# A two-layer program on one core: routing one attention body nearer, one activation table, pads on two queues, expert weights scaled on ScalarE

## What is computed

```python
h = layernorm(x) * (1 + ca) + sa
q = softplus(h @ Wq.T + bq); k = softplus(h @ Wk.T + bk); v = h @ Wv.T + bv      # 16 heads of 8
kv = cumsum(k[..., :, None] * v[..., None, :]); k1 = cumsum(k)
x = x + ga * ((q . kv) / (q . k1)) @ Wo.T + ...
h = layernorm(x) * (1 + cb) + sb
t = h * rsqrt(mean(h * h) + 1e-5) * norm_scale
top_v, top_i = top_k(t @ gate_w + gate_b, 2); probs = softmax(top_v)
for each expert e:  acc += w[:, e] * (swiglu(t @ w1[e] + b1[e]) @ w2[e] + b2[e])
x = x + gb * (h + acc)
```

## Time and profile before

| | us |
|---|---|
| median of 3 runs | 1131.31 (1131.22 to 1132.76) |
| profiled execution, first to last instruction | 1130.5 |
| layer 0 | 0 to 404 |
| attention and routing, bodies overlapping | 404 to 753 |
| run-out: routing of the last bodies | 753 to 797 |
| pads, plan, last scatters | 797 to 818 |
| expert stage | 818 to 1091 |
| sum and store | 1091 to 1131 |

### The profile page before, as it was taken

The page is one execution under the profiler, slowest core; times in us unless marked ns, Lnnn a source line. Parts: engine busy times, 40 slices in busy tenths (PEclk is TensorE's granted clock), DMA queues, the critical chain, the costliest instruction groups (busy, mean ns, idle before and its releaser), DMA issues.

```text
span 1130.5 us, 21078 instructions
## 1 busy us (share of the span) xinstructions
PE 904.8 (80%) x6543; PEld 700.5 (62%) x6543; DVE 863.6 (76%) x2224; ACT 682.1 (60%) x1756; POOL 563.3 (50%) x567
## 2 busy tenths in 40 slices
PE   4997799279999949999999999942088888888820
PEld 4994377134445438888888888831077777777710
DVE  2776788789998866788999999955467777676748
ACT  1357510689996376688988987755055555555510
POOL 1121000656885224433888888856635655555530
PEclk9999899579999969999999999975589999999975
DMA  7000233123333132000101111111242222222148
GB/s 191 14 1 5 75 112 112 52 85 132 123 118 113 75 102 51 2 8 9 42 32 39 38 37 40 35 37 45 82 131 72 82 71 77 79 68 77 45 165 307
DMA packets 72002, 84.37 MB, mean 75 GB/s; under 512 B 18182, under 2 KB 59841, under 8 KB 69716
## 3 DMA queue, kind: packets, MB, share of 16 engines
q1 hardware_dynamic: 52564, 60.60, 17.1%
q0 software_dynamic: 8704, 18.11, 4.8%
q10 hardware_dynamic: 10624, 4.33, 1.4%
HBM read 59.33 MB, written 23.67 MB: 73 GB/s over the span
## 4 chain that ended last, share of the span: by engine, by line
PE 39%; DVE 9%; issue 5%; ACT 4%; another core or an unknown queue 3%; DMA 1%; SPq 1%; POOL 0%; DVEq 0%; ACTq 0%; POOLq 0%
PE ps L2086 9%; PE ps L2304 9%; PE ps L2102 3%; PE ps L2323 3%; DVE qk L2003 2%; PE ps L2077 1%; PE ps L2064 1%; PE ps L2051 1%; PE ps L2097 1%; PE ps L2191 1%; PE ps L2156 1%; PE ps L2145 1%; PE ps L2209 1%; DVE qk L2008 1%
## 5 line engine op out<-in xcount | busy, mean ns | idle before, releaser
L1399 POOL DMA_INDIRECT rows_of<-payb,posu x128 | 143.2, 1119 | 53.3 <-issue 28.7
L1390 POOL TENSOR_TENSOR kvb<-qk,v 128x1024 f32<-128x1024 f32 x64 | 126.4, 1980 | 86.4 <-DVE qk L1756 53.0
L1032 PE MATMUL ps<-masked,ew 128*128 128x512 f32 x256 | 129.6, 621 | 4.2 <-DVE masked L960 3.5
L2086 PE MATMUL ps<-con,kvb 128*128 128x128 f32 x1024 | 126.9, 278 | 0.0
L2086 PEld LDWEIGHTS ps<-con,kvb 128*128 128x128 f32 x1024 | 120.4, 193 | 0.7 <-issue 0.7
L1424 POOL DMA_INDIRECT parts<-h,dest x72 | 74.0, 1028 | 72.3 <-ACT h L1658 47.2
L1649 ACT ACTIVATE nrm<-qk 128x512 f32<-128x512 f32 x72 | 45.4, 630 | 101.3 <-DVE qk L2003 87.8
L1424 POOL DMA_INDIRECT parts<-gx,dest x72 | 73.6, 1022 | 55.0 <-ACT gx L1658 33.9
L960 DVE TENSOR_TENSOR masked<-f_t,wide 128x512 f32<-128x512 f32 x128 | 88.9, 712 | 9.2 <-PE ps L1032 8.9
L1732 DVE TENSOR_TENSOR qc<-ps,qk 128x1024 f32<-128x1024 f32 x64 | 77.9, 1217 | 18.1 <-PE ps L2086 17.7
L2304 PE MATMUL ps<-qd,ex 128*128 128x256 f32 x288 | 74.4, 405 | 18.0 <-ACT ex L1634 15.8
(11 more groups left out here) (355 smaller groups left out, 2444.1 us busy)
## 6 DMA issues: line engine op xcount, KB each, us to landing
wide<-hot_dram SPq DMA_DIRECT2D x16, 1024.0 KB, 4.6
kvb<-rows_of SPq DMA_DIRECT2D x72, 132.0 KB
toep<-taps_dram SPq DMA_DIRECT2D x16, 512.0 KB, 3.8
out_dram<-x_tok ACTq DMA_DIRECT2D x16, 256.0 KB, 5.6
rows<-rows_dram SPq DMA_DIRECT2D x16, 192.0 KB, 3.1
kvb<-parts SPq DMA_DIRECT2D x6, 512.0 KB, 7.2
rows<-rows_dram SPq DMA_DIRECT2D x16, 128.0 KB, 4.4
xg<-in_w_dram SPq DMA_DIRECT2D x1, 2048.0 KB, 9.7
```

What stands on the lines that cost most here:

```text
L1032: nc.tensor.matmul(ps[:, w % 2, :], ew0[:, e, :], masked[e % 4][:, :], start=False, stop=(e == E - 1)).then_inc(s["product"], 1)
L1390: nc.gpsimd.tensor_tensor(kv[g % KB][:, :, :].rearrange("p e (h d) -> p e h d", h=H), k_in, v_in, ALU.mult).then_inc(s["kv"], 1)
L1399: nc.gpsimd.indirect_dma_start(rows_of, bass.IndirectOffsetOnAxis(ap=posu[w % 2][:, slot, t:t + 1], axis=0), pay[w % PB][:, t, :], None).t ...
L2086: last = nc.tensor.matmul(cum(g)[:, e, :], kv[g % KB][:, e, :], k("upto"), start=True, stop=True)
```

## The change

1. **Order of the loops.** The calls from `payload` on (payload, turned payload, logits, choice, ranks, places, sends) get an offset smaller by one: ACT `payload(n - 7)`, `logits_kept(n - 8)`, `weigh(n - 8)`; DVE `logits(n - 5)` to `placed(n - 5)`; PE `turn_pay(n - 5)`, `logits(n - 5)`, `ranks(n - 6)`, `logits_back(n - 6)`; POOL `send(n - 5, ...)`. Each loop has one pass less. PE's waits on shared PSUM banks are counted as they are issued, instead of by formulas with `upto_b`, and name two more semaphores; two of ACT's waits name the readers of `qk` one by one.
2. **One table.** ACT preloads the set `natural_log_exp_and_others` at the block's start; `variance_root` and `square_root` move up behind their logarithms.
3. **Pads.** SP writes 4 of the 8, ACT the other 4, each behind `place` = 1.
4. **Weights and tables.** ACT scales two experts' first weights in each of four passes (n = 7 to 10); the bias and `beside` are made by DVE in its pass n = 4 (`numbers`). The plan loses these, and one of its links: `cnt` is now computed straight from PSUM beside `base`.

```diff
@@ block.sync
-                    for e in range(E):
+                    for e in range(E // 2):
@@ block.gpsimd
-                    for n in range(B + 7):
-                        send(n - 7, 6)
+                    for n in range(B + 6):
+                        send(n - 6, 6)
                         products(n, 0)
-                        send(n - 7, 7)
-                        send(n - 6, 0)
+                        send(n - 6, 7)
+                        send(n - 5, 0)
...
@@ block.scalar
+                    def scaled_weights(q):
+                        need(act, "experts", (2 + NF) * 16)
+                        act.wait_ge(s["weights"], 3 * 16)
+                        by_e = w1b1.rearrange("p (e i) -> p e i", i=WB)[:, 2 * q:2 * q + 2, 0:I2]
+                        nc.scalar.activation(by_e, by_e, ACT.Copy, scale=ns[:, :]).then_inc(s["scaled"], 1)
...
-                    for n in range(B + 9):
+                    nc.scalar.preload_act_table_set("natural_log_exp_and_others")
+                    for n in range(B + 8):
                         abs_keys(n - 3)
...
                         variance_log(n - 6)
-                        logits_kept(n - 9)
+                        variance_root(n - 6)
+                        logits_kept(n - 8)
                         squares(n - 7)
                         logarithm(n - 3)
                         square_log(n - 7)
+                        square_root(n - 7)
                         projected(n - 5)
                         feat(n - 2)
-                        variance_root(n - 6)
-                        weigh(n - 9)
+                        weigh(n - 8)
                         spread(n - 4)
-                        payload(n - 8)
-                        square_root(n - 7)
-                        turned_pay(n - 8)
+                        payload(n - 7)
+                        turned_pay(n - 7)
...
+                        if 5 <= n - 2 <= 8:
+                            scaled_weights(n - 2 - 5)
+
+                    act.wait_ge(s["place"], 1)
+                    act.wait_ge(s["padrow"], 2)
+                    for e in range(E // 2, E):
+                        row = act.value_load(counts[0:1, e:e + 1], min_val=e * CAP, max_val=(e + 1) * CAP - SP)
+                        act.dma_start(rows_of[bass.ds(row, SP), :].rearrange("(p c) d -> p c d", c=S), far[:, :, :]).then_inc(s["pads"], 16)
                     act.wait_ge(s["place"], 2)
+                    need(act, "scaled", E // 2)
@@ block.vector
-                    for n in range(B + 6):
+                    for n in range(B + 5):
...
-                        logits(n - 6)
-                        largest(n - 6)
-                        chosen(n - 6)
+                        logits(n - 5)
+                        largest(n - 5)
+                        chosen(n - 5)
...
+                        if n == 4:
+                            numbers()
...
+                    nc.vector.tensor_scalar(cnt[:, :], ps[:, RANK, 0:E], float(SP - 1), None, ALU.add)
...
-                    link(nc.vector.scalar_tensor_tensor(cnt[:, :], k("iota"), float(-CAP), base[:, :], ALU.mult, ALU.add))
-                    link(nc.vector.tensor_scalar(cnt[:, :], cnt[:, :], float(SP - 1), None, ALU.add))
...
-                    first_weights = w1b1.rearrange("p (e i) -> p e i", i=WB)[:, :, 0:I2]
-                    nc.vector.tensor_scalar(first_weights, first_weights, ns[:, :], None, ALU.mult)
@@ block.tensor
-                    for n in range(B + 7):
-                        logits_back(n - 7)
+                    for n in range(B + 6):
+                        logits_back(n - 6)
...
-                        ranks(n - 7)
+                        ranks(n - 6)
                         sums(n - 2, 3)
-                        turn_pay(n - 6)
+                        turn_pay(n - 5)
```

More of the change, by code:

```diff
@@ L1173, in build @@
                      "pay", "pay_ps", "pay_t", "gx", "x4", "lg_ps", "lg_t", "lg_back", "lg", "max", "idx", "idf", "hot", "ed", "ee", "e1", "p1", "taken", "counted", "carried",
-                     "rank_ps", "rank", "sel", "pos", "posu", "extra", "labels", "totals", "base", "place", "pads", "experts", "plan", "padrow")
+                     "rank_ps", "rank", "sel", "pos", "posu", "extra", "labels", "totals", "base", "place", "pads", "experts", "plan", "padrow", "beside", "scaled")
             s = {nm: sem(f"p3_{nm}") for nm in names}
@@ L1934, in _ @@
                     link(nc.vector.tensor_tensor(first[:, :], upto[:, :], ntile[:, :], ALU.subtract))
-                    dve.wait_ge(s["experts"], (2 + NF) * 16)
-                    lin_bias = w1b1.rearrange("p (e i) -> p e i", i=WB)[:, :, I2 + NF // 2:WB]
-                    nc.vector.tensor_scalar(lin_bias, lin_bias, 1.0, None, ALU.add)
-                    first_weights = w1b1.rearrange("p (e i) -> p e i", i=WB)[:, :, 0:I2]
-                    nc.vector.tensor_scalar(first_weights, first_weights, ns[:, :], None, ALU.mult)
+                    need(dve, "beside", 3)
                     nc.vector.tensor_scalar(surplus[:, :], number[:, :], last_tile[:, :], NOWHERE, ALU.is_gt, ALU.mult)
-                    for half in range(S):
-                        last = nc.vector.tensor_scalar(beside[:, :, half], number[:, :], float(SP), k("token")[:, half:half + 1], ALU.mult, ALU.add)
-                    link(last)
-                    link(nc.vector.tensor_scalar(beside[:, :, :], beside[:, :, :], float(2 * TILES * P), None, ALU.add))
                     link(nc.vector.tensor_scalar(number[:, :], number[:, :], last_tile[:, :], None, ALU.min))
@@ L2036, in _ @@
                 def _(pe):
+                    issued = dict.fromkeys(("turned", "queries", "states", "denominators", "keys", "spread", "projected", "turn_pay", "ranks", "values", "first_cum", "back", "logits", "logits_back"), 0)
                     def keys(w):
@@ L2058, in queries @@
                                 pe.wait_ge(s["first"], 3 * 16)
[L2059 to L2062 removed]
+                            need(pe, "abs_q", issued["queries"])
+                            need(pe, "relu_q", issued["queries"])
+                            need(pe, "rden", issued["denominators"])
+                            need(pe, "feat", issued["turned"])
+                            need(pe, "ds", issued["states"])
+                            issued["queries"] += 1
                             need(pe, "feat", w + 1)
@@ L2107, in turned @@
                         if exists(w):
-                            need(pe, "relu_q", upto_b(w))
-                            need(pe, "rden", upto_b(w - 1))
-                            need(pe, "feat", upto_b(w))
-                            need(pe, "ds", upto_b(w - 1))
+                            need(pe, "abs_q", issued["queries"])
+                            need(pe, "relu_q", issued["queries"])
+                            need(pe, "rden", issued["denominators"])
+                            need(pe, "feat", issued["turned"])
+                            need(pe, "ds", issued["states"])
+                            issued["turned"] += 1
                             need(pe, "nrm0", w + 1)
@@ L2272, in _ @@
                         sums(n - 1, 1)
-                        logits(n - 6)
+                        logits(n - 5)
                         projected(n - 2)
+                    need(pe, "pay_t", B)
+                    need(pe, "wo_t", B)
                     need(pe, "rank", B)
```

169 lines of the change are left out of this document (97 added, 72 removed).

## The result

| | kernel before | changed kernel |
|---|---|---|
| median, us | 1132.76 (1131.22 to 1138.93, 7 runs) | 1122.98 (1120.92 to 1129.91, 7 runs) |
| ratio, 95% interval | | 0.9898 (0.9869 to 0.9927) |
| profiled execution: time, span | 1131.3, 1130.5 | 1129.91, 1127.9 |

The changed kernel is 1.0% faster. 0.9898 of the 1131.3 us from which I forecast is 1119.8: a gain of 11.5 us, where I had said 14.8; the two medians lie 9.8 us apart. The median itself, 1122.98, lies 1.0 us above the range that I gave.

A forecast was written before the change was run, and what follows sets the result against it. PE bounds the attention stage; POOL's sends set the first tile load, moving it from 818.4 to 803.7 (-14.7 us). With -0.1 for the preload, 1131.3 - 14.8 = 1116.5 us, range 1111 to 1122.

The forecast's parts named there:

- the signs that I had named: Profile after: periods 20.6 us, body 12 sent near 760, first tile load near 803.7, following neither pads nor plan.
- Routing one body nearer: POOL behind the last product: 44 sends instead of 52; the last 32 need 41.4 us, where 40 took 56.39.
- The pads' 1.6 us: Ahead of the first tile load: the pads end last, costing 1.6 us more than POOL alone would.
- Body 12's first send: POOL in the run-out: comes at 760.2, from 758.34 plus 1.7 for a full period and 0.2 for ACT's root.
- Rival (b): ACT's 4.20 us idle stall before body 11's logits doesn't recur, body 12 is sent earlier: 1112.3 us; chance 0.07.
- Counts: Run-out: written at 785.5 instead of 796.9, with 6.4 us of table loads gone; at 791.9 if other waits replace them.
- Pads and plan: Ahead of the first tile load: pads land at 797.7, plan done at 799.4, both before POOL ends at 801.6.
- rival (a): Pads or plan set the first tile load's start: 1121.1 us, or 1124.1 if ACT issues pads slowly; chance 0.11.
- Cover of the steady stage: Attention stage: ACT's four weight scalings lie under cover because PE bounds there, costing nothing.
- Rival (c): Steady stage: payload comes too late for PE, full periods grow; 1134.1 us if 2.3 us later; chance 0.05.
- Rival (d): Run-out keeps its length, the passes left taking the dropped one's work: 1131 us; chance 0.04.
- The two rules: Trainium skill: DVE's weights pass locks out POOL's sends (1.7 us gone for good); table switches add 1.38 us drain, sum unmoved.

The follow-up runs named there:

- calm pair: Changed kernel and kernel before, both unedited, in surroundings where the kernel before takes 1073 us: 1064.06 us against 1073.17, ratio 0.9924.
- run 3: Kernel before with one activation table alone (preload, both roots right behind their logarithms): ratio 1.0014.
- run 7: Changed kernel with table loads back, all 8 pads from SP and first weights scaled by DVE, against the kernel before: ratio 0.9912.
- run 12: Kernel before, unedited, profiled for comparison with run 11: span 1070.3 us; beside run 11 the kernel before took 1073.17 us.
- run 11: Changed kernel, unedited, against the kernel before: 1064.06 us, ratio 0.9924.
- disturbed: Surroundings in which the kernel before took 1129 to 1137 us, where it takes 1073 us in calm ones.
- run 1: Changed kernel, unedited, for a second profile, against the kernel before: 1118.66 us, ratio 0.9906.
- run 4: Changed kernel with POOL's scatters of bodies 11 to 15 held until DVE's plan is done, and more posu buffers: 1145.74 us, one run.
- run 8: Changed kernel with four of body 11's eight scatters held until body 12 is ranked, against the kernel before: ratio 0.9893.
- run 2: Changed kernel with table loads back (no preload, both roots behind the exponentials again), against the kernel before: 1120.21 us, ratio 0.9913.
- run 5: Changed kernel with all 8 pads issued by SP, against the kernel before: ratio 0.9934.
- run 6: Changed kernel with the first weights scaled by DVE inside the plan again, against the kernel before: ratio 0.9918.
- runs 9 to 12: Changed kernel with POOL memsets ahead of body 11's sends (0.9915) or those of bodies 11 to 15 (0.9924), then run 11 and run 12.

## Why the prediction was right, and where it was off

The mechanism held: the gain comes from eight sends less behind the last product. The calm pair shows it, where POOL sets the start in both kernels and the move of the start, 9.66 us, is the whole gain (the spans differ by 9.5). The ratios of runs 3 and 7 agree: one table alone gives nothing (1.0014), routing nearer alone gives 0.9912, as much as all parts together (0.9898, 0.9906, 0.9924). The size was 3 to 5 us too large. Term by term, in the calm pair (runs 12 and 11), and in the disturbed profiles (first of before, run 1):

| term | forecast | calm pair | disturbed |
|---|---|---|---|
| preload, fill of the pipeline | -0.1 | -1.6 (body 0's query to body 2's: 32.32, 30.73) | -2.7 |
| one more full period | +1.7 | +1.4 | +3.3 |
| first send of the run (body 11 before, 12 after) | +1.9 | +0.8 | +6.8 |
| length of the run of sends | -15.0 | -10.3 (53.17, 42.87) | -13.4 |
| POOL's end to the first tile load | -1.6 | -0.1 (2.47, 2.33) | -0.9 |
| sum of the last three, at the first tile load | -14.7 | -9.7 | -7.5 |

What was measured of the first two terms lies within the third and isn't added again; in the forecast the preload's -0.1 stood apart. The disturbed profiles can't serve for the sum: their expert stages took 262.2 to 272.6 us with the same instructions (268.76 in run 1, 272.59 before), where I had given that stage nothing.

That the ratio fell into the range is in part luck. By the signs that I had named, the first profile spoke against me: the first tile load followed the plan, body 12 went at 765.48, full periods were 20.5 to 20.9 us with one of 21.76, and the start had moved by 1.5 us. Run 1's has POOL at the start, but body 12 late too (765.09).

*The step that was mis-sized* is the one under "Routing one body nearer": 40 sends in 56.39 us. It held a wait of 2.83 us for body 13's ranks, which I subtracted from the mean of a send but left in the length that goes away. It doesn't exist in the calm kernel before, where the 40 sends run in 53.17 us without a wait. Eight sends of 1.288 us ((53.17 - 1.65) / 40) are 10.3; the long send's 1.65 goes too, and is eaten by other sends that take 1.2 to 1.5 us (seven of the last 32, where the kernel before has one beside the long one), so that the 32 take 1.340 each.

*The pads' 1.6 us* was the second. That they ended last in the profile of before was true of that execution alone. Their spacing of 2.15 us was itself disturbance: in the calm kernel before the eight are issued in 8.06 us, 1.0 each. I took one execution's waits for properties of the kernel.

*Body 12's first send*, forecast for 760.2, came at 765.48 and 765.09 in the disturbed profiles. In the calm pair it comes 48.47 us after the last query, body 11's before 47.30, so it is only 1.2 us later. Rival (b) asked whether the stall of 4.20 us goes; it grew to 6.19 and 6.70, and beside a kernel before of 1129 to 1137 us only silent POOL (run 4) or four held sends (run 8) removed it. Taking it away alone gains nothing that shows: run 8's ratio is 0.9893.

*Counts* were to move by -11.4 us. The calm pair has -8.9 (781.51 to 772.59). Of the five loads on the chain, 6.4 us in my sum, three lie in the passes from body 12 to 15; they are worth 1.6 us there (25.24, 23.68) and 2.3 in run 2, where 3.8 would be their own length; other waits took their time, as my own bound allowed. It moved nothing, since POOL bounds.

*Pads and plan* ahead of POOL: right in run 1 and in run 11, wrong in the first profile, where the counts came at 799.37 and the plan took 16.4 us instead of 13.9. That is rival (a), to which I gave 0.11. It is no property of the changed kernel either: the same plan takes 6.8 us in run 11 (772.76 to 779.53), and before it was 10.3 (781.68 to 792.02).

*Cover of the steady stage.* The scaled weights were not quite free: 1.07 us in one period in the disturbed profiles (run 5's 21.77 against run 6's 20.70), 0.15 in run 11 (20.50 against 20.35). Rival (c) didn't occur: the full periods are 20.35 in both. Rival (d), no change, is refuted by the result and by run 7's ratio. The expert stage kept its length in the calm pair: 227.60 and 227.86 us.

*The two rules.* DVE's pass over the weights and the long send belong together: 2.61 us in run 12, 2.76 in run 6, 2.79 in run 7, and none over 1.46 behind the last product in the changed kernel. The Trainium skill, "SBUF — State Buffer", section "SBUF: two separate sides", says that a vector operation in a two-port mode keeps GpSimd from writing the descriptors of its DMAs. The trace agrees in that the long send stands beside the pass each time; no row shows the port mode of the pass. The pass isn't the only thing that lengthens a send: in the attention stage one send of nearly each body takes 1.8 to 2.4 us in both kernels, as at 585.31 in run 11 (2.30 us), beside a pass of DVE over `lg` and `ex` of 1.16. The drain of 1.38 us per switch that "ScalarE: Activation LUTs", section "What ACT_TABLE_LOAD costs", adds (the Trainium skill too) shows in no run: four loads less in the bodies 0 and 1 gave 1.6 us, three less in the run-out 1.6 to 2.3, both under the 1.28 that each row itself lasts.

What stays open: what the surroundings are. They lengthen waits, and the issue of the pads, on every engine but POOL; in the run-out they need POOL's sends for it, as far as the one execution of run 4 shows; the records don't name the source. No run tests routing nearer alone in calm surroundings. No version that I ran beats the changed kernel by more than the intervals allow, so I offer none.

## What to carry to other kernels

Before a wait that one profile shows is put into a sum as a thing that goes away, look whether it is the kernel's: take a second profile, or ask whether an instruction on the same engine, waiting for its own predecessor, shows waits of the same size. If it does, the waits are disturbance, and the sum should hold only counts times durations (here 8 sends of 1.29 us). Where one engine's queue of issues bounds a run-out, take issues off that engine; shortening the neighbours' chains (tables, pads, plan) gives nothing that can be measured here, though in single executions pads (run 5) or plan (first profile) can come last.

## What the runs showed of the hardware

- With POOL issuing indirect DMAs one after another (0.96 us each, 1.26 apart), every other engine can stop starting instructions: 5.3 to 6.2 us inside eight sends in a row (body 11's, in run 3 body 10's) in the first profile of after and in those of runs 1, 2, 3, 5, 6 and 7, ending some 1.4 us after the last of them in run 1 (755.88, then 757.26). With POOL silent in the same surroundings (run 4, one execution): none. In the surroundings of runs 9 to 12: none either, with the same sends. In these runs it took both.
- The transfers themselves are not what is late: in runs 1, 4 and 8 and in the first profile of after a send's first packets start 1.5 to 2.1 us after the send does, within a hold-up or outside.
- The waits come in steps: starts on DVE in the first profile of after lie at 799.37, 802.16, 803.57, 804.97, 806.37 and 810.57, which are multiples of 1.40 us apart.
- The expert stage took 262.2 to 272.6 us in the ten disturbed profiles and 227.6 to 228.5 in the four calm ones, with the same instructions.
- A kernel's time can differ by 5 to 6% (1129 to 1137 us and 1073) with the same instructions, while the ratio of two kernels hardly changes (0.9898, 0.9906, 0.9924).
